# Layer 0's adapter heads: turned sixteen in a block and put on their rows by transfers, with four identity products ahead of the turn of the experts' input

## What is computed

```python
# adapter attention of layer 0: 32 heads of width 8
q = split_heads(hidden_states @ Wq, q_len)
k = split_heads(hidden_states @ Wk, q_len)
v = split_heads(hidden_states @ Wv, q_len)
q = q * cos + _rotate_half(q) * sin
k = k * cos + _rotate_half(k) * sin
scores = jnp.einsum('bhqd,bhkd->bhqk', q, k) * inv_sqrt_d      # 32 heads, contraction over 8
...
a_k = split_heads(adapter @ Wk, adapter_len)                  # keys of the context
a_v = split_heads(adapter @ Wv, adapter_len)
a_scores = jnp.einsum('bhqd,bhkd->bhqk', q, a_k) * inv_sqrt_d  # 32 more sets of scores
```

## Time and profile before

| | |
|---|---|
| median of 3 runs | 1411.72 us (1411.42 to 1414.34) |
| the profiled execution | 1412.15 us, its span 1410.4 us |
| mean granted PE clock | 0.972 of full speed |
| PE busy | 1269.5 us, 90% of the span |
| DVE busy | 1046.1 us, 74% |
| ACT busy | 675.6 us, 48% |
| POOL busy | 135.1 us, 10% |
| transfers | 86.12 MB, q1 (SP's queue and others of its kind) 25.7% of 16 engines' span |

### The profile page before, as it was taken

The page is one execution under the profiler, slowest core; times in us unless marked ns, Lnnn a source line. Parts: engine busy times, 40 slices in busy tenths (PEclk is TensorE's granted clock), DMA queues, the critical chain, the costliest instruction groups (busy, mean ns, idle before and its releaser), DMA issues.

```text
span 1410.4 us, 25548 instructions
## 1 busy us (share of the span) xinstructions
PE 1269.5 (90%) x9658; PEld 894.1 (63%) x9658; DVE 1046.1 (74%) x2349; ACT 675.6 (48%) x1286; POOL 135.1 (10%) x223
## 2 busy tenths in 40 slices
PE   6979999999999999999999999989899868788886
PEld 3747666766766766676676676656677735554544
DVE  5768588588677857857767775654788878889877
ACT  2326335534633643543463364352344348888752
POOL 2210020010011001001001100000000011122101
PEclk9979999999999999999999999999999979999998
DMA  7331001000200200200020023000400159999910
GB/s 235 160 105 62 13 4 46 30 12 16 63 12 16 63 12 12 66 13 1 16 63 12 12 63 120 19 24 0 102 9 9 31 103 176 170 166 176 176 23 30
DMA packets 176121, 86.12 MB, mean 61 GB/s; under 512 B 138240, under 2 KB 170368, under 8 KB 175744
## 3 DMA queue, kind: packets, MB, share of 16 engines
q1 hardware_dynamic: 174848, 84.13, 25.7%
q10 hardware_dynamic: 1152, 0.36, 0.1%
HBM read 43.57 MB, written 5.24 MB: 35 GB/s over the span
## 4 chain that ended last, share of the span: by engine, by line
PE 64%; DVE 19%; issue 5%; ACT 5%; DMA 4%; POOL 1%; ACTq 0%; DVEq 0%; POOLq 0%; SPq 0%
PE ps_t L1892 12%; PE ps_p L1876 11%; PE ps_s L2125 8%; PE ps_o L2042 5%; PE ps_o L2032 4%; PE ps_o L1957 4%; DMA w_moe<-w_moe 4%; PE ps_o L2125 3%; PE ps_p L1934 3%; DVE w_moe L1780 3%; DVE probs L1277 2%; PE ps_s L1934 2%; PE ps_o L1961 2%; DVE row_max L1283 1%; PE ps_p L2407 1%
## 5 line engine op out<-in xcount | busy, mean ns | idle before, releaser
L1892 PE MATMUL ps_t<-ident,probs 128*128 128x128 f32 x1072 | 170.4, 280 | 28.6 <-ACT probs L1067 8.0
L927 ACT ACTIVATE probs<-probs 128x512 f32<-128x512 f32 x184 | 115.6, 628 | 136.8 <-DVE probs L1277 136.8
L1892 PEld LDWEIGHTS ps_t<-ident,probs 128*128 128x128 f32 x1072 | 123.2, 142 | 78.1 <-issue 37.9
L889 ACT ACTIVATE probsT<-ps_t 128x512 f32<-128x512 f32 x232 | 136.5, 589 | 64.0 <-PE ps_t L1892 63.9
L2125 PE MATMUL ps_s<-w_moe,xbT 128*128 128x352 f32 x352 | 121.9, 471 | 0.0
L1876 PE MATMUL ps_p<-w_qkv,xinT 128*128 128x512 f32 (+1 forms) x240 | 106.8, 570 | 10.3 <-DMA xinT<-in_xT 7.5
L833 POOL TENSOR_TENSOR rms<-mean_sq,neg_half 128x8 f32<-128x8 f32 x40 | 67.1, 1678 | 270.4 <-DVE mean_sq L1311 270.4
L2407 PE MATMUL ps_p<-ident_b 128*128 128x256 bf16 x512 | 85.3, 293 | 0.0
L889 ACT ACTIVATE bigT<-ps_t 128x512 f32<-128x512 f32 (+1 forms) x128 | 68.9, 553 | 33.3 <-PE ps_t L1892 31.3
L2125 PEld LDWEIGHTS ps_s<-w_moe,xbT 128*128 128x128 f32 x352 | 64.1, 194 | 22.0 <-issue 1.4
L1957 PE MATMUL ps_o<-v_all,probsT 128*128 128x128 f32 x512 | 70.7, 282 | 6.6 <-DVE big L1341 6.2
(11 more groups left out here) (344 smaller groups left out, 2784.4 us busy)
## 6 DMA issues: line engine op xcount, KB each, us to landing
w_out<-in_wT_out SPq DMA_DIRECT2D x8, 2048.0 KB, 8.8
w_moe<-in_wT_gu SPq DMA_DIRECT2D x1, 5632.0 KB, 18.2
w_moe<-in_wT_down SPq DMA_DIRECT2D x1, 2816.0 KB, 10.6
keys<-keys2T SPq DMA_DIRECT2D x8, 256.0 KB, 2.0
keys2T<-keys SPq DMA_DIRECT2D x4, 512.0 KB, 10.7
w_moe<-w_moe SPq DMA_TRANSPOSE x128, 3.4
w_qkv<-in_wT_qkv SPq DMA_DIRECT2D x3, 512.0 KB, 4.9
w_qkv<-in_wT_qkv SPq DMA_DIRECT2D x1, 1536.0 KB, 8.2
```

The costliest lines, as they stand in the source:

```text
L889: nc.scalar.activation(dst, src.bitcast(BF16) if dst.dtype == BF16 else src, ACT.Copy)\
L927: nc.scalar.activation(probs[:, at % 4, :], probs[:, at % 4, :], ACT.Exp).then_inc(L0.exped, 1)
L1892: ins = nc.tensor.transpose(dst[:, i * P:(i + 1) * P], src(i), ident_b[:] if bf else ident[:])
```

## The change

The heads are no longer padded. The adapter's query and key weights are reordered on the host, so that 16 heads of 8 fill a block of 128 columns in such an order that after the turn the rows 8a to 8a+7 of each block, inside each quarter of 32 rows, are the head of place a. PE turns 4 blocks for q and k (before 16) and 2 for the context keys (before 8), in one batch each, and ACT moves each batch once (before four and two times), to the staging places `qk_turned` (the last quarter of `big`) and `ak_turned` (the last half of `kdup`). From there 16 transfers on SP's queue for each of the two put 8 rows each on rows 0, 32, 64 and 96 on of `bigT` and `akT`. The heads phase waits for both sets (`ld_qk`, `ld_ak`), and DVE waits for them before it writes `kdup` (c = 0) and the last quarter of `big` (c = 4) for the next tile. Last, four products of the bfloat16 identity with itself, 512 columns each, whose result nobody reads, stand between `v2` and the turn of `xb`, in tiles 0 to 6.

```diff
-AFTER = {0: [("x1",)], 1: [("qkx",)], 2: [("vx",)], 3: [("k",), ("qk", 0), ("qk", 1)],
-         4: [("qk", 2), ("qk", 3), ("h", 0)], 5: [("q0",), ("d", 0)], 6: [("q1",), ("h", 1)], 7: [("kT",), ("d", 1)],
+AFTER = {0: [("x1",)], 1: [("qkx",)], 2: [("vx",)], 3: [("k",), ("qk",)],
+         4: [("h", 0)], 5: [("q0",), ("d", 0)], 6: [("q1",), ("h", 1)], 7: [("kT",), ("d", 1)],
...
-        qk_pad = big[:, 0:2 * HX * PAD].rearrange("p (h d) -> p h d", d=PAD)
+        kdup_words = kdup[:].rearrange("p a b c -> p (a b c)")
+        qk_flat, ak_flat = big[:, 0:4 * P], kdup_words[:, 0:2 * P]
+        qk_turned = big[:, 12 * P:16 * P].rearrange("p (b t) -> p b t", b=4)
+        ak_turned = kdup_words[:, 2 * P:4 * P].rearrange("p (b t) -> p b t", b=2)
...
+            def spread(dst, src, signal):
+                dst = dst.rearrange("p (b a) t -> p b a t", a=4)
+                for at in range(4):
+                    for quarter in range(4):
+                        first = PAD * quarter
+                        sp.dma_start(dst[first:first + HDX, :, at, :], src[first + HDX * at:first + HDX * (at + 1)])\
+                            .then_inc(signal, 16)
+
+            sp.wait_ge(L0.trans_taken, T0.done(0, ("ak", 0)))
+            spread(akT[:], ak_turned, ld_ak)
...
+                if 0 < n < TILES:
+                    sp.wait_ge(L0.trans_taken, T0.done(0, ("ak", n)))
+                    spread(akT[:], ak_turned, ld_ak)
                 if n < TILES:
                     sp.wait_ge(L0.proj_taken, P0.done(0, ("v2", n)))
                     sp.dma_start(values_dram[n], value_tile).then_inc(values_stored, 16)
                 if m < TILES:
                     sp.dma_start(ctxT[:], a["ctxT"][m]).then_inc(ld_ctx, 16)
+                if n < TILES:
+                    sp.wait_ge(L0.trans_taken, T0.done(0, ("qk", n)))
+                    spread(qkT, qk_turned, ld_qk)
...
-                    dve.wait_ge(L0.trans, T0.done(0, ("qk", t - 1, 3) if c else ("ak", t - 1, 1)))
+                    dve.wait_ge(L0.trans, T0.done(0, ("qk" if c else "ak", t - 1)))
+                    if c == 0:
+                        dve.wait_ge(ld_ak, 16 * 16 * t)
+                    elif c == 4:
+                        dve.wait_ge(ld_qk, 16 * 16 * t)
...
             def ak_transposes(n):
                 pe.wait_ge(L0.proj_taken, P0.done(0, ("ck", n)))
-                for i in range(2):
-                    transpose(L0, ("ak", n, i), lambda q: padded(ak_pad, 16 * i + 4 * q), 4)
+                transpose(L0, ("ak", n), lambda i: ak_flat[:, i * P:(i + 1) * P], 2)
-            def qk_transposes(n, j):
+            def qk_transposes(n):
                 pe.wait_ge(qkx_ready, n + 1)
-                transpose(L0, ("qk", n, j), lambda i: padded(qk_pad, 16 * j + 4 * i), 4)
+                transpose(L0, ("qk", n), lambda i: qk_flat[:, i * P:(i + 1) * P], 4)
...
-                taken(L0, ("qk", b, 3))
+                pe.wait_ge(ld_ak, 16 * 16 * (b + 1))
+                pe.wait_ge(ld_qk, 16 * 16 * (b + 1))
...
                     project(L0, ("v2", n), ctxT, w_kv2, D, D)
+                    dense(ps_s[:, 0, :], 4)
```

More of the change, by code:

```diff
@@ L141, in transposes0 @@
         keys += [("b", b, 3), ("ox", b)]
-        keys += [("ak", n, 0), ("ak", n, 1)] if n < TILES else []
+        keys += [("ak", n)] if n < TILES else []
         keys.append(("x2", b))
@@ L152, in transposes0 @@
                 elif what == "qk":
-                    keys.append(("qk", n, *j))
+                    keys.append(("qk", n))
                 elif what == "kT":
@@ L460, in decoder @@
         second_q = opening_words[:, 24 * P:40 * P]
-        qk_pad = big[:, 0:2 * HX * PAD].rearrange("p (h d) -> p h d", d=PAD)
+        kdup_words = kdup[:].rearrange("p a b c -> p (a b c)")
+        qk_flat, ak_flat = big[:, 0:4 * P], kdup_words[:, 0:2 * P]
+        qk_turned = big[:, 12 * P:16 * P].rearrange("p (b t) -> p b t", b=4)
+        ak_turned = kdup_words[:, 2 * P:4 * P].rearrange("p (b t) -> p b t", b=2)
         qkT = bigT[:, 0:16, :]
-        ak_pad = kdup[:].rearrange("p a b c -> p (a b c)").rearrange("p (h d) -> p h d", d=PAD)
         vx, avx = (w[:, 0:HX * (HDX + 1)].rearrange("p (h d) -> p h d", h=HX) for w in (vx_wide, avx_wide))
@@ L532, in decoder @@
         ld_kv2 = sem("ld_kv2")
+        ld_qk, ld_ak = sem("ld_qk"), sem("ld_ak")
         ld_const = sem("ld_const")
@@ L948, in x1_evac, with qk_evac @@
                 evac(L0, ("x1", n), flat(xT[1][:]), D)
-            def qk_evac(n, j):
-                evac(L0, ("qk", n, j), flat(qkT[:, 4 * j:4 * j + 4, :]))
+            def qk_evac(n):
+                evac(L0, ("qk", n), flat(qk_turned))
             def ak_evac(n):
-                for i in range(2):
-                    evac(L0, ("ak", n, i), flat(akT[:, 4 * i:4 * i + 4, :]))
+                evac(L0, ("ak", n), flat(ak_turned), 2 * P)
             def c_evac(n):
@@ L1004, in beside_experts @@
                         elif what == "qk":
-                            qk_evac(n, j[0])
+                            qk_evac(n)
                         elif what == "h":
@@ L1049, in opening @@
                 square(1, 4)
-                for j in range(4):
-                    qk_evac(0, j)
+                qk_evac(0)
                 q0_evac(1, 2)
@@ L1390, in rotate_x @@
                 dve.wait_ge(L0.proj_taken, P0.done(0, ("qkx", n)))
-                nc.vector.tensor_tensor(qk_pad[:, :, 0:HDX], heads(ropes[:, 0, :], 2 * HX),
+                nc.vector.tensor_tensor(heads(qk_flat, 2 * HX), heads(ropes[:, 0, :], 2 * HX),
                                         heads(ropes[:, 1, :], 2 * HX), ALU.add).then_inc(qkx_ready, 1)
@@ L1486, in beside_experts @@
                 if following:
-                    take(("ck", n), ak_pad[:, :, 0:HDX], HX)
+                    take(("ck", n), heads(ak_flat, HX), HX)
                     take(("cv", n), avx[:, :, 0:HDX], HX)
@@ L1569, in opening @@
                 dve.wait_ge(L0.trans, T0.done(0, ("k0", 0, 1)))
-                take(("ck", 0), ak_pad[:, :, 0:HDX], HX)
+                take(("ck", 0), heads(ak_flat, HX), HX)
                 take(("cv", 0), avx[:, :, 0:HDX], HX)
@@ L2142, in beside_experts @@
                         elif what == "qk":
-                            qk_transposes(n, j[0])
+                            qk_transposes(n)
                         elif what == "h":
@@ L2224, in opening @@
                 project(L0, ("vx", 0), xT[1], w_x, 2 * D, D)
-                for j in range(4):
-                    qk_transposes(0, j)
+                qk_transposes(0)
                 project_in(1, "v")
@@ L2466 @@
 _OUT = (TILES, P, D)
-_DIRECT = ["L0_attn_q_norm_w", "L0_attn_k_norm_w", "L0_xattn_Wq", "L0_xattn_Wk", "L0_xattn_Wv", "L0_xattn_Wo",
+_DIRECT = ["L0_attn_q_norm_w", "L0_attn_k_norm_w", "L0_xattn_Wv", "L0_xattn_Wo",
            "L1_attn_b_qkv", "L1_attn_b_out", "L1_xattn_Wq", "L1_xattn_bq", "L1_xattn_Wkv", "L1_xattn_bkv",
@@ L2501, in lay_out @@
     arrays = {n: np.ascontiguousarray(g[n]) for n in _DIRECT}
+    for name in ("L0_xattn_Wq", "L0_xattn_Wk"):
+        arrays[name] = np.ascontiguousarray(g[name].reshape(D, 2, 4, 4, HDX).transpose(0, 1, 3, 2, 4).reshape(D, D))
     arrays["x"] = np.ascontiguousarray(g["x"])
```

2 lines of the change are left out of this document (1 added, 1 removed), and 4 rows, old and new, of the table OPENING_TURNS.

## The result

The changed kernel took 1410.80 us in the median of 13 runs (1407.78 to 1412.04), and the kernel before, run beside it on the same chip, 1414.34 (13 runs, 1410.70 to 1419.93): a ratio of 0.9976, 95% interval 0.9967 to 0.9985. By the ratio that is 3.4 us less (2.1 to 4.7), by the medians 3.5: a quarter of a percent, but clear of the noise. The forecast was 1409.0, with a difference of -2.75.

What follows compares the result with a forecast made beforehand. PE and DVE were taken to meet at the turn of q3, with PE alone bounding tile 6. Terms -0.3 - 1.8 - 0.65 + 1.7 - 3.4 + 1.7 = -2.75 us gave a median of 1409.0, range 1403 to 1419.

Steps and rivals of the forecast that it cites:

- The bound: Tiles 0 to 5: PE and DVE meet at the turn of q3; fewer PE transposes gain only 0.3 us.
- Tile 6: Experts of tile 6, where PE is the bound: fewer transposes and a vanished wait gain 1.8 us.
- The joint's cover: Ahead of xb: PE arrives 0.22 us later, covered by its 0.83 us wait for DVE's norm, so costs nothing.
- The opening: Before the first scores: six fewer transposes gain 0.65 us; waiting for the q and k transfers costs 1.7 us.
- the room for `kdup`: DVE's write of kdup: the context keys' transfers land with 1.5 us to spare, at 0.64 us per issue.
- Rival C: Ahead of kdup: transfers land late above a 0.74 us pitch and DVE waits; 1427.5 us at 0.90, chance 0.15.
- The clock at the joints: Joints of tiles 0 and 4: the identity products remove two falls of PE's clock, gaining 3.4 us.
- The clock elsewhere: Behind the turn of q3: one new clock fall, +1.7 us; heads phases: perhaps a few falls fewer, not summed.
- The sum: Whole kernel: the terms make -2.75 us on the profiled 1412.15, forecasting a median of 1409.0 us.
- A: Full tiles: PE is the bound after all, so 1.76 us counts in each of six; 1398.5 us, chance 0.08.
- B: Turn of q3: the clock falls at the new wait in most tiles, 8.5 us more; 1417.5 us, chance 0.12.
- D: Identity products leave the clock falls as they were; 1410.7 us, or 1412.4 with the new fall; chance 0.2.

Runs made afterwards that it cites:

- the swap: DVE does pieces of layer 1's context keys ahead of scale_heads, in its wait for POOL: changed kernel so altered 1405.30 us, kernel before so altered 1407.49 us.
- e5_after_fill: Changed kernel with seven more identity products in PE's wait ahead of the turn of q3, tiles 0 to 5: 1407.78 us, ratio 0.9964 to the kernel before.
- e7_loads_first: Changed kernel with the akT transfers issued behind those of values and ctxT, in every tile but the first: 1418.51 us, ratio 1.0035 to the kernel before.
- the split opening: Changed kernel with 8 of the first tile's 16 q and k transfers issued from ACT's queue: 1406.94 us, ratio 0.9955 to the kernel before.
- e11_after_heads_fill: Changed kernel with identity products in the two waits for ACT's exponentials at each heads phase's start, from tile 1 on: 1405.91 us.
- e1_before_products: Kernel before with only the four identity products ahead of the turn of xb, tiles 0 to 6: 1403.30 us, ratio 0.9936.
- e9_swap_split_fill: Changed kernel with context keys ahead of scale_heads on DVE, half the opening's q and k transfers on ACT's queue, identity products in heads-phase waits: 1390.47 us.
- e3_before_swap: Kernel before with DVE doing pieces of layer 1's context keys ahead of scale_heads, in its wait for POOL: 1407.49 us, ratio 0.9960.

## Why the prediction was right, and where it was not

**The bound.** Right. PE's slack at the turn of q3 was taken as 0.05 us and 0.3 us as the gain of six tiles. Measured: undisturbed tiles of 116.25 to 116.31 us before and 116.25 to 116.30 after, between which 0.05 us can't be told, and q3's turn waits 1.73 us (said: 1.76). The fill and the swap, together, show that this wait is slack and DVE's chain the cause. Of DVE's five waits ahead of the heads, one in the trace before (1.08 us at 535.85) is put down to a turn of PE and not to POOL; in the changed kernel the same wait, 1.08 us, is put down to POOL, so the premise that PE doesn't feed this chain stands.

**Tile 6.** Said 1.8 us; measured 1.84 (103.22 to 101.38, with the products in both).

**The joint's cover.** Right. The four products cost nothing; the wait ahead of `xb` is 0.62 us (said: about 0.6).

**The opening.** The mechanism was right, and the size off. Said +1.7 - 0.65 = 1.05 us; measured 2.34 later, with a wait of 2.65. The term was mis-sized by the pitch of issues: 0.64 us from the row for transfers of 64 rows, where 8 rows took 0.73. Fifteen times 0.09 is 1.35. With it the estimate is 2.4. Of the 0.65 us that the six missing transposes were to give, 0.51 arrived at the turn of `big` (83.02 against 83.53). The same pitch made the room for `kdup` 0.43 us and not 1.5. Rival C said that DVE would wait for the transfers of `akT`, in every tile; in the changed kernel it doesn't, but the room is gone in tile 0, where the issues took 0.5 us longer, and it was exceeded in one tile of `e5_after_fill`.

**The clock at the joints.** Right in kind: two falls gone, 1.00 at all seven joints. Tile 4 gained 1.68 us and tile 0 1.18 net, against 1.7 each.

**The clock elsewhere.** This step failed. The sum had one new fall, +1.7, behind the turn of q3, and left the heads phases to a remark on the chances. In fact the kernel before had falls there in two tiles: tile 5, 118.90 - 116.26 = 2.6 us, and tile 6, 104.53 - 103.22 = 1.3. Both were absent from the trace after, and one stood in tile 1, 1.5 us. That is -2.4 us where the sum had +1.7. These falls come at the waits for ACT's exponentials, and filling the wait at the turn of q3 did not take them away.

**The sum.** To the first scores of tile 7 the change saved 904.00 - 899.14 = 4.9 us (said: 2.75). The rest of the span, which it doesn't touch from the end of tile 7's experts on, took 506.4 us before and 510.4 after in the profiled pair. In the thirteen runs of each the difference was 3.4 to 3.5. The number agrees with the forecast partly by luck. In layer 0 the clock gave 4.1 us more than the sum had (-2.4 for +1.7) and the opening 1.3 less, and in the profiled pair the rest of the span, which the sum had at nothing, took 4.0 back. That the products alone came out 7.5 us lower than the whole change follows from no term of the sum.

**The rivals.** A fell: the full tile did not shorten. It named its own condition, that DVE's waits for POOL shrink; under it (the swap) the gain came, 1.95 us a tile. B fell for this kernel: no fall stands behind the turn of q3. Its mechanism exists, though, and not far away: at waits of 2.25 to 2.51 us, in `e7_loads_first`, two of six tiles show it. D, that the products leave the falls as they were, fell at the joints. Its time, 1410.7, is nearer to the measured 1410.80 than the forecast's 1409.0, but both were counted from 1411.72; against the 1414.34 run beside it, the difference of -3.5 is nearer to -2.75 than to D's -1.0.

**What stays open.** The rest of the span ranges over the traces from 504.1 to 514.1 us, in code that is the same but for tile 7's share, and it follows the clock. Windows of nearly the whole rest, first of the kernel with the split opening, then of `e11_after_heads_fill`:

```profile
894.00:1408.00 514.00, 438.39 (x3742) 293.98 (x3740) 401.35 (x764) 280.29 (x497) 52.58 (x156) 0.93 0.47 83
```

```profile
897.00:1403.00 506.00, 430.89 (x3742) 288.85 (x3742) 400.49 (x764) 279.51 (x497) 52.95 (x156) 0.96 0.47 85
```

The same work, and 0.03 in the granted clock goes with 8 us. Why one kernel gets more low time in layer 1 than another, no run here tells; the 15 us of low time between `e1_before_products` and the changed kernel belong here, and so do 5.6 us of the gain of `e9_swap_split_fill`. Open too are the fewer falls of `e3_before_swap`, and why one set of transfers landed 1.6 us late.

## What to carry to other kernels

Where two engines arrive together, work taken from one becomes a wait of equal length, and shows its worth only when the other's chain is cut as well: test both cuts together, not one by one, before either is judged. When transfers replace compute, count the queue's time per issue with the nearest row as a lower bound, since fewer rows did not issue faster here, and leave the first user a microsecond or two of room: 0.43 us was used up in tile 0 and exceeded once by 1.2. Short waits on PE that lie between transposes and thin products are worth filling with identity products even when the wait itself costs nothing: behind two waits of 0.70 and 0.57 us the clock fell in some tiles, at 1.0 to 1.5 us each in most, and not once when they were filled. And time the smallest part of a change by itself: here one line, the four products, did better than the whole.

## What the runs showed of the hardware that was not expected

- A transfer of 8 rows from on-chip to on-chip memory takes the issuing queue 0.73 us from one issue to the next, more than one of 128 rows to or from outside (0.47) or of 64 rows on chip (0.64). ACT's queue needs the same, but 1.55 us for the first (8 in 6.83 us). Both queues issue at once.
- The granted clock fell to its lower level in heads phases where PE had no wait above 0.70 us from the first scores on. Five identity products, 1.1 us, kept it at 1.00 in all heads phases that had them. The Trainium skill (TensorE: Matmul & The Clock Gate, "Part 4: PE-mode transpose") states that a transpose doesn't count as busy as other products do; what preceded the falls fits that, but no run here replaced the transposes alone.
- A set of 16 transfers that takes 12.94 us from its first issue to its use once took some 1.6 us more, with the issues at their usual pitch; and in tile 0 of every trace with packed heads the issues of a set took 0.4 to 1.1 us more than in the other tiles.
